# Value products of the first attention: four key tiles in one group, a fifth step behind the scores, in place of two and four

## The reference, cut to what matters

```python
    q = jnp.concatenate([q_content, q_rope], axis=-1)
    k = jnp.concatenate([k_content, k_rope], axis=-1)
    scores = jnp.einsum('bhqd,bhkd->bhqk', q, k) * scale
    scores = jnp.where(causal[None, None], scores, jnp.float32(-jnp.inf))
    attn = jax.nn.softmax(scores, axis=-1)
    out = jnp.einsum('bhqk,bhkd->bhqd', attn, v)
```

## Time and profile before

| what | value |
|---|---|
| time, median of 3 runs | 1527.55 us (1525.64 to 1531.12) |
| span of the profiled execution, first to last instruction | 1519.5 us |
| median less this span | 8.05 us |
| PE / DVE / ACT / POOL busy over the span | 83% / 76% / 55% / 45% |
| mean granted TensorE clock | 0.899 |

### The profile page before, as it was taken

How to read it: one execution, slowest core, us unless ns; L and a number is a source line. 1 busy time by engine, 2 the same in 40 slices (tenths; PEclk the granted TensorE clock), 3 DMA queues, 4 the chain that set the end, 5 groups by cost and what they waited for, 6 DMA issues and landing times.

```text
span 1519.5 us, 38187 instructions
## 1 busy us (share of the span) xinstructions
PE 1254.7 (83%) x13524; PEld 854.0 (56%) x13524; DVE 1153.3 (76%) x3936; ACT 832.7 (55%) x2003; POOL 690.7 (45%) x1043
## 2 busy tenths in 40 slices
PE   5489899998899888999888899959988999557780
PEld 2344444445455454454444799947777778546660
DVE  5588787897898977989875755547799988755666
ACT  1145456554555544555556545438887767326663
POOL 3023232333233333324313454556687888674664
PEclk9689999998999989999999989977898877568995
DMA  4665726557266472573770221021111112222335
GB/s 112 102 104 83 117 36 94 90 84 117 32 89 113 62 120 36 84 127 47 122 221 28 83 59 37 22 65 45 45 46 47 54 51 75 94 73 79 89 87 172
DMA packets 73886, 123.25 MB, mean 81 GB/s; under 512 B 17534, under 2 KB 46083, under 8 KB 72800
## 3 DMA queue, kind: packets, MB, share of 16 engines
q1 hardware_dynamic: 63896, 104.97, 36.4%
q0 software_dynamic: 7616, 13.59, 2.8%
q10 hardware_dynamic: 2184, 2.25, 0.7%
HBM read 30.40 MB, written 17.60 MB: 32 GB/s over the span
## 4 chain that ended last, share of the span: by engine, by line
PE 39%; DVE 31%; issue 10%; POOL 8%; ACT 7%; DMA 4%; DVEq 1%; SPq 0%; ACTq 0%; POOLq 0%
DVE first L833 5%; PE A L632 5%; PE S L1099 5%; PE S L615 4%; PE S L604 4%; DVE S L836 4%; DMA Qp<-mT 2%; DVE tA L812 2%; POOL xq L1468 2%; PE A L1106 2%; PE S L1659 2%; DVE tB L813 2%; PE S L596 2%; PE S L194 2%; PE A L1670 2%
## 5 line engine op out<-in xcount | busy, mean ns | idle before, releaser
L717 ACT ACTIVATE P<-S 128x512 f32<-128x512 f32 (+3 forms) x768 | 333.4, 491 | 286.2 <-PE S L615 281.8
L907 POOL TENSOR_SCALAR_AFFINE_SELECT P<-P 128x256 f32<-128x256 f32 (+1 forms) x256 | 116.5, 459 | 390.2 <-ACT P L717 390.1
L615 PE MATMUL S<-Qp,Kp 121*128 121x512 f32 (+3 forms) x768 | 254.8, 396 | 35.1 <-DVE tB L813 9.6
L604 PE MATMUL S<-Kp,Qp 120*128 120x512 f32 (+3 forms) x768 | 255.0, 402 | 33.1 <-DMA Kp<-big 16.1
L836 DVE CUSTOM_DVE_ANT_0 S<-S,later 128x512 f32<-128x512 f32 (+3 forms) x512 | 239.0, 512 | 44.3 <-PE S L604 43.1
L604 PEld LDWEIGHTS S<-Kp,Qp 120*128 120x128 f32 x768 | 136.0, 199 | 168.0 <-issue 76.3
L615 PEld LDWEIGHTS S<-Qp,Kp 121*128 121x128 f32 x768 | 141.1, 195 | 111.4 <-issue 24.1
L833 DVE TENSOR_REDUCE first<-S 128x1 f32<-128x512 f32 x256 | 164.3, 683 | 48.8 <-PE S L604 48.6
L632 PE MATMUL A<-P,V 128*9 128x512 f32 (+3 forms) x1536 | 176.6, 508 | 5.1 <-POOL P L907 5.0
L2264 POOL DMA_INDIRECT yq<-yq,id x71 | 70.4, 991 | 51.5 <-DVE id L2221 23.2
L1896 POOL TENSOR_TENSOR prod<-mid,kT 128x128 f32<-128x128 f32 x160 | 68.2, 460 | 51.0 <-ACT mid L1727 34.4
(11 more groups left out here) (358 smaller groups left out, 2637.3 us busy)
## 6 DMA issues: line engine op xcount, KB each, us to landing
Qp<-big SPq DMA_DIRECT2D x63, 256.0 KB
Kp<-big SPq DMA_DIRECT2D x62, 256.0 KB
Qp<-big SPq DMA_DIRECT2D x63, 128.0 KB
Kp<-big SPq DMA_DIRECT2D x62, 128.0 KB
xq<-xq SPq DMA_DIRECT2D x71, 72.0 KB, 1.9
yb<-yq SPq DMA_DIRECT2D x8, 528.0 KB, 7.1
big<-in_w SPq DMA_DIRECT2D x4, 1024.0 KB, 9.6
big<-vt SPq DMA_DIRECT2D x32, 128.0 KB
```

The lines of the kernel that those rows point to most:

```text
L604: te.matmul(S[s][:, 512 * h:512 * h + n], Q[0:120, h, 128 * qt:128 * qt + 128], K[0:120, h, 512 * part:512 * part + n], start=True, stop=T ...
L615: te.matmul(S[s][:, 512 * h + c:512 * h + 512], K[0:121, h, 128 * kb:128 * kb + 128], Q[0:121, h, 512 * qh + c:512 * qh + 512], start=True ...
L717: se.activation(k.P[(w.n - 1) % NP0][:, h, c:512], S[s][:, 512 * h + c:512 * h + 512], ACT.Exp, scale=SCALE0).then_inc(p.done("st").h, 1)
L907: ge.affine_select(P[:, :, start:c + 128], P[:, :, start:c + 128], [[0, 2], [1, wide]], ALU.is_ge, 0.0, base=start - c, channel_multiplier ...
```

## The change

`pend` is emptied four key tiles at a time, when it holds five, so each `pv` item has 8 matmuls instead of 4, and there are 96 of them instead of 192. The counts that other engines wait for are halved with it; the six buffers `P` stay.

```diff
-LAG = 4
+LAG, FLUSH = 5, 4
 NP0 = 6
...
         def flush():
-            two = (pend.pop(0), pend.pop(0))
-            u, qh, kb = two[1].at[:3]
-            o.add("pv", u, qh, two)
+            some = tuple(pend.pop(0) for _ in range(FLUSH))
+            u, qh, kb = some[-1].at[:3]
+            o.add("pv", u, qh, some)
             if kb == 4 * qh + 3:
                 tails.append(tail(u, qh))
...
-            pe.wait_ge(p.done("st"), 2 * two[1].n)
-            if diagonal(two[1]):
-                pe.wait_ge(p.sem("g_causal"), diagonal(two[1]))
-            for e in two:
+            pe.wait_ge(p.done("st"), 2 * some[-1].n)
+            if diagonal(some[-1]):
+                pe.wait_ge(p.sem("g_causal"), diagonal(some[-1]))
+            for e in some:
...
-                act.wait_ge(p.made("pv"), 48 * (w.n - 2))
+                act.wait_ge(p.made("pv"), 24 * (w.n - 2))
...
-                act.wait_ge(p.made("pv"), (w.n - NP0 + 1) // 2)
+                act.wait_ge(p.made("pv"), (w.n - NP0 - 1) // FLUSH + 1)
...
-            act.wait_ge(p.made("pv"), 6 * u + (6 if qh else 2))
+            act.wait_ge(p.made("pv"), 3 * u + (3 if qh else 1))
```

More of the change, by code:

```diff
@@ L617, in attn0_tensor @@
         elif w.kind == "pv":
-            u, qh, two = w.at
+            u, qh, some = w.at
             oa = (2 * u + qh) % 2
```

## The result

The changed kernel takes 1662.54 us (median of 4 runs, 1651.55 to 1669.48), the kernel before beside it 1526.60: ratio 1.0879 [1.0831, 1.0927]. It is slower, as forecast, but by some 134 us where 42 were reckoned, and outside the range. The profiled execution has a span of 1649.8 us, 130.3 more than before. Its own time was 1651.55 us, so only some 1.8 us lie around the instructions; most of the 8.05 us that the forecast added to its span is the scatter between executions.

The account below looks back on a forecast made before the run. Neither PE nor VectorE was free; which one limits changes from unit to unit. Terms 9.5 + 7.9 + 18 + 3.5 + 3.2 = 42 us, the 20.2 saved included, on 1527.55 gave 1570 us, range 1522 to 1602.

Parts of the forecast that it names:

- What goes: Flushes of PE: three fewer in a unit save 0.63 us, over 32 units 20.2 us.
- A and C: Groups of value products for steps 0 to 3 and 8 to 11; each to last 1.40 us on PE.
- B: Group of value products for steps 4 to 7; to last 1.83 us on PE.
- the joins: 96 places where a group's second four weights follow its first four matmuls; taken as 0, bounds 0 to 10.6 us.
- What is put at risk on VectorE: VectorE rests behind A, B and C, together 3.40 us a unit; 9.5 us for rotation units, 7.9 for quiet ones behind.
- the units behind: Seven quiet units following rotation units: VectorE's rest goes from 2.27 to 3.40 us, 7.9 us in all.
- The unit's end: Twelve other quiet units near the transfer: a flush moves behind the `st` and VectorE starves, 1.5 us each, 18 us.
- third rival: In all units, added rests come on top of most present ones: 70 us plus 6.6 of low clock, 1604 us; chance 0.14.
- Nearness priced at 0, or 10 us if the cover is gone: At B the product awaits step 7's exponential; hidden by the wait for piece 9, else 0.3 us a unit.
- the five heaviest: Five units with the heaviest projections, which rest anyway: 0 to 1.5 us each, 0.7 taken, 3.5 us.
- The clock, 3.2 us: PE's longer waits for the transfer put one further unit at the low clock: 3.2 us.
- the first two: Rivals: PE sets the pace, 1507 us, chance 0.14; or rests and savings meet, 1523 to 1532 us, chance 0.10.

Follow-up runs that it names:

- e3: Kernel before, still emptied in pairs but with three pending: flushes after even steps, newest exponential one step old; 1583.20 us, ratio 1.0385.
- e1: Against the kernel before, groups of four instead of pairs at the old distance (six pending), flushes after steps 1, 5 and 9; 1597.17 us, ratio 1.0473.
- e2: Kernel before, still in pairs but emptied when five are pending: flushes after even steps, newest exponential three steps old; 1550.97 us, ratio 1.0193.
- e10: The change with only half of the columns of each value product computed; 1595.97 us, ratio 1.0443 to the kernel before.
- e13: Groups of four emptied at six pending, flushes after steps 1, 5 and 9, with half of each value product's columns; 1545.44 us, ratio 1.0118 to the kernel before.
- e11: The kernel before with only half of the columns of each value product computed; 1504.31 us, ratio 0.9835.
- e8: Against the kernel before, groups of four emptied at seven pending: flushes after steps 2, 6 and 10, newest exponential three steps old; 1611.45 us, ratio 1.0558.
- e4: The change with the rotation work one step earlier, no longer right behind a flush; 1633.57 us, ratio 1.0705 to the kernel before.
- e12: The kernel before with the rotation work one step earlier, which puts it right behind flushes; 1545.81 us, ratio 1.0121.
- e5: The change with ten added matmuls, results overwritten, in each rotation unit where PE waited; 1649.12 us, ratio 1.0780 to the kernel before.

## Why the prediction was wrong

Size, the step from e3 to the change, makes 0.0494 of the 0.0879 measured; e1 has 0.0473 for it. Places and nearness together, from the kernel before to e3, make the other 0.0385. Their split by e2 (0.0193 and 0.0192) does not hold for the change, because e2 has the collisions and the change has none. By the forecast's own steps:

- **What goes**: right. A and C were to take 1.40 us and B 1.83, and at the full clock, counted to the next `mx`, 35 groups take 1.39 to 1.40 us and 25 take 1.83 to 1.84. So the joins cost nothing: with 0.11 us a join, A and C would have taken 1.51. The Trainium skill, "TensorE: Matmul & The Clock Gate", section "The mechanism" of Part 3, has it that a weight load overlaps running matmuls only where its row group differs. The trace does not agree: all four column blocks use the same rows, and in the group at 893.68 us the later weights load while its first matmuls run. With 0.11 us a join the sum would still have been 80 us short.
- **What is put at risk on VectorE**: the right mechanism, wrongly sized, and this is the step that failed. The sentence "a rotation unit goes from 2.05 us of rest to 3.40" came out at 9.83 in the unit shown, and the term of 9.5 us for seven of them at 51.5, the largest miss of the sum. The 7.9 us for the units behind measured 17.5. The formula priced each gap behind a group alone, at the full clock, and took the present rests off in full. It left out the other half of the same thing: with no product for four steps, PE runs ahead into the ring of three and waits there (8.2 to 56.0 us), and that time is missing when the block comes. The gaps of a quiet unit at full clock came out nearest (4.23 us for 3.40). e10 and e13, each against e11, show that the length of the block matters, and that it is not all. How the remaining 2.8% divide between PE's waits, VectorE's gaps and the clock is argued from the rows, not shown.
- **The unit's end**: waits for the transfer rose to 14.4 us from 8.6, as said. The forecast's 12 other units grew by 29.5 us for the 18 reckoned, 2.46 us a unit; that is closer to its third rival, which has 2.27. The last unit, put at 0, grew by 5.8 us with the projection behind it.
- **Nearness priced at 0, or 10 us if the cover is gone**: wrong. The products' waits for GpSimd's masks and ScalarE's exponentials are 15.4 us in the change (8.8 + 6.6) and 29.9 in e3, before 5.0. With pairs it measured 29 us (e3 against e2), 16.8 of it in the six units with projections, but e2's collisions stand in that difference. For the five heaviest the forecast had 3.5 us in all, and they grew by 21.8; by e1 and e8 size and nearness both have a part in that.
- **Places**: half seen. That rotation right behind a flush takes VectorE's cover away was in the working, without a price of its own. Taking the rotation out from behind the flush gains 1.7% in the change (e4). The price with pairs is not settled: in e2 and e12 the collisions of L862 with L895 stand beside it, 18.9 and 10.8 us.
- **The clock, 3.2 us**: the low clock rose from 46 to 150 us over the 31 units. Filling PE's waits in the rotation units is worth at least 16 us there. The forecast looked only at the waits for the transfer and not at the ring.
- **The rivals**: the first two fell with PE's and VectorE's waits both growing. The third, rests on top in all units, was the nearest with 70 us, and still half of what came.
- The later stages last the same within their scatter, as said. No version tried that computes everything beats the kernel before.

## What to carry to other kernels

Where two engines feed each other through a short ring, both halves of a regrouping have a price: compare the longest block with the work the ring holds for the other engine, and the longest stretch without one with the entries that are free, and do it in the busiest units, not in a quiet one. A gap formula fitted to a quiet unit gave 1.4 us where the busiest units lost 7. Change size, distance and place one at a time: here size cost 75 us, and distance and place together 59. And look at what else such a run has moved: e2 was to measure the places alone and brought two engines into collision.

## What the runs showed of the hardware

- Matmuls for two more key tiles join a group without a gap although their weights go to column blocks in use: 1.39 to 1.40 us for 16 records where 0.11 us a join would have made it 1.51.
- A VectorE multiplication of two SBUF tensors (L862) that begins while a GpSimd operation on SBUF (L895, 2.37 us) is at work ends only 0.08 to 0.09 us after it: 1.68 to 2.24 us instead of 0.22, ten times in e2, seven in e12 and twelve in e8. VectorE's reciprocal with one input, and its reductions from PSUM, keep their length beside L895 (0.20 and 0.68 us).
- The clock fell without any long wait. In the rotation unit shown PE waited 0.69, 0.53 and 0.27 us between 795 and 798.5 us and 0.76 us up to 799.86; the granted clock was 0.93 over the stretch to 800 us and 0.50 behind it. The kernel before did so too, at fewer places: it went to 0.50 at 693.1 us after waits of 0.20, 0.81 and 0.21 us. So a wait of 2.70 us is not needed for it. The 10 matmuls more in each rotation unit of e5 took the low clock in these units from 62.8 to 10.4 us.
